# A graph aggregation with layer norm on one core: gathered rows split twice per four groups instead of four times, and the ring of copied indices taken out

## The chip, the cores and the metric

One core of one Trainium2 chip runs the kernel. The metric is device microseconds of one launch, the median of three runs; the program before takes 1273.84 us (1270.81 to 1276.02).

## The reference, cut to what matters

`x` has 100,000 rows of 128 float32, and there are 50,000 edges (`src`, `dst`). The output is a layer norm over each row of x plus the summed messages of its edges:

```python
row, col = (edge_index[0], edge_index[1])            # row = src, col = dst
messages = jnp.einsum('ei,oi->eo', x[col], W) + b
out = jax.ops.segment_sum(messages * agg_weight, row, num_segments=x.shape[0])
x = _layernorm(x + out, axis=-1)
```

So each edge adds row x[dst], times W, plus b, to node src. The sum over the rows is made first and multiplied by W after it, and b is added as often as the node has edges (its degree).

## The kernel before, in words

The first part of the program (about 244 us of the profiled span) sorts the edges into a **table** of 441 lists of up to 128 edges. Its last step, `decode` (L894 to L903), turns the sorted words into two int32 of each entry: the row of x to gather (`table[:, c, 0]`) and the node's column within a window (`table[:, c, 1]`). It does so for the first 36 lists (`head`), and then for the rest.

The second part goes over 196 **groups** of 512 nodes (the last one has fewer). Four groups are one **period**, and a period has 9 lists, so there are 49 periods. A list spans up to 308 nodes, so it can serve two neighbouring groups. The code calls g the group, u its place in a ring, m = period modulo RX (RX = 4) the ring place of the gathered rows. The engines work as follows.

- GpSimd (POOL) issues for each list one indirect DMA that gathers 128 rows of x into `xg[:, m, k]` (L516). The row numbers come from `now`, a ring of 4 periods that VectorE fills with a copy of 9 table entries (`fetch`, L968; the first four at L960). The copy for a period is made 13 rounds ahead of the period's first group and waits until the matmuls have released the ring place; POOL waits for the copy (`s_idx`).
- VectorE (DVE) splits the gathered float32 rows into three bf16 parts. The upper half of each word is the first part; `rest` = xg minus that part (L980); `xl` = rest minus rest's upper half (L985). Between these, one comparison for each list builds `sel` (L982), the 0/1 matrix of edges by nodes. These three steps are `select`. `CLASS` gives for each of a period's groups the lists that start there: 3, 2, 3 and 1. `select` runs once per group, for 384, 256, 384 and 128 columns, and up to 6 groups ahead of the group that is being finished (`lead`).
- TensorE (PE) sums the rows of each node: three matmuls for each list and group (L696, L698, L700), and for two groups at a time a degree matmul (L710), after which `s_agg` rises by 2. This is `aggregate`. `project`, two groups behind, adds b by degree (L723) and the product with W (L726), and signals `s_out`.
- ScalarE (ACT) copies the sums out of PSUM (L1094) and for every odd group the degrees of two groups (L1097); three groups behind it takes the square root (`std`, L1101), and four groups behind it writes the normalised output `y` (four instructions, L1107).
- VectorE's **round** g is: `add_x` (h = bank times aw plus x, 128x512, L991, waits for `s_out`), `select` for a later group, `moments` (four bn_stats of h, L997, which wait for h by `s_h`), `invert` of g - 1 (L1007, waits for ACT's std), `combine` (four bn_aggr, L1003), and `recentre` of g - 1 (L1011).
- SyncE loads x by group into `xt` and stores `y`, with rings of 8.

The order on each engine is that in which the code is written; the engines meet by semaphores alone. This is VectorE's order:

```python
lead = lambda g: min(6, 4 + g // 4)
for g in range(lead(0)):
    one(select, g)
for g in range(GA + 1):
    one(fetch, g + 13)
    one(add_x, g)
    for ahead in range(g + lead(g), g + 1 + lead(g + 1)):
        one(select, ahead)
    one(moments, g)
    one(invert, g - 1)
    one(combine, g)
    one(recentre, g - 1)
```

## Time and profile before

| what | value |
|---|---|
| median of three runs | 1273.84 us |
| span of the profiled execution | 898.2 us |
| around the span (median less span) | 375.6 us |
| first gather to the last | 245.2 to 855.5 us |
| DVE busy over the span | 853.2 us (95%) |
| PE / ACT / POOL busy | 735.0 / 656.6 / 592.8 us (82 / 73 / 66%) |
| granted TensorE clock, mean | 0.949 |

The profile gives the span from the first to the last instruction of one execution and no second time for the same execution; what the device time has beyond it is taken as the difference to the median. Two successive instructions of DVE overlap in the trace: the first one's duration reaches beyond the start of the second. So what an instruction costs its engine is read from start to start, and the duration only says when its result is there.

### The profile page before, as it was taken

How to read it: one execution, taken by the hardware profiler on the slowest of the kernel's cores; microseconds unless marked ns; L12 is line 12 of the kernel's file. 1: busy time of each engine (PE TensorE's matmuls, PEld its weight loads, DVE VectorE, ACT ScalarE, POOL GpSimd, SP SyncE). 2: the span in 40 equal slices, each digit the busy share in tenths (PEclk: the TensorE clock that was granted, in tenths of full speed). 3: DMA queues.
4: the chain of work that ended last, by engine and by line, in shares of the span. 5: the costliest groups of instructions: out<-in, count | busy, mean ns of one | idle time of the engine just before them, and what ended most of it. 6: DMA issues, size and time to landing. Idle time of an engine off the chain costs nothing.

```text
span 898.2 us, 24417 instructions
## 1 busy us (share of the span) xinstructions
PE 735.0 (82%) x7822; PEld 549.6 (61%) x7849; DVE 853.2 (95%) x3877; ACT 656.6 (73%) x1690; POOL 592.8 (66%) x601
## 2 busy tenths in 40 slices
PE   4889999999978778787877887879778787797874
PEld 3735555555456666666766676657666666675664
DVE  7989999999959999999999999999999999999997
ACT  2157777777526777777887778777777787878778
POOL 3047777776477777777777777776777777777710
PEclk9999999999999999989999999998999989989898
DMA  2001111110225677676666766676666666666653
GB/s 74 24 15 38 38 38 38 38 38 26 87 82 166 206 217 213 213 220 215 212 215 207 212 210 212 208 215 204 205 209 217 210 211 206 215 208 211 210 182 120
DMA packets 81035, 141.18 MB, mean 157 GB/s; under 512 B 19360, under 2 KB 20396, under 8 KB 80908
## 3 DMA queue, kind: packets, MB, share of 16 engines
q1 hardware_dynamic: 62476, 110.55, 36.7%
q0 software_dynamic: 18432, 29.08, 13.4%
q8 instruction: 63, 1.03, 0.5%
q14 instruction: 64, 0.52, 0.2%
HBM read 87.64 MB, written 51.92 MB: 155 GB/s over the span
## 4 chain that ended last, share of the span: by engine, by line
DVE 66%; PE 22%; issue 7%; ACT 2%; POOL 2%; DMA 0%; SPq 0%; ACTq 0%; DVEq 0%; POOLq 0%
DVE stats L997 16%; DVE h L991 11%; DVE sel L982 10%; PE bank L648 9%; DVE rest L980 8%; DVE xl L985 7%; DVE mv L1003 7%; PE bank L542 2%; PE bank L597 2%; PE bank L726 2%; PE bank L603 2%; ACT y L1107 1%; POOL xg L516 1%; PE bank L612 1%; DVE rstd L1007 1%
## 5 line engine op out<-in xcount | busy, mean ns | idle before, releaser
L516 POOL DMA_INDIRECT xg<-in_x,now x441 | 448.7, 1018 | 173.1 <-issue 132.5
L1107 ACT ACTIVATE y<-h,shift,rstd 128x128 f32<-128x128 f32 x784 | 320.2, 479 | 0.1
L726 PE MATMUL bank<-wT,aggT 128*128 128x128 f32 x1568 | 242.2, 301 | 0.0
L726 PEld LDWEIGHTS bank<-wT,aggT 128*128 128x128 f32 x1568 | 203.4, 203 | 28.4 <-issue 11.9
L696 PE MATMUL bank<-sel,xg 128*128 128x308 bf16 (+11 forms) x685 | 170.3, 261 | 7.6 <-DVE xl L985 7.6
L698 PE MATMUL bank<-sel,rest 128*128 128x308 bf16 (+11 forms) x685 | 176.4, 261 | 0.0
L479 POOL DMA_INDIRECT place_scratch<-word_col,place_row x135 | 135.7, 1005 | 55.4 <-issue 50.1
L997 DVE BATCH_NORM_STATS2 stats<-h 128x6 f32<-128x128 f32 x784 | 168.9, 275 | 0.2
L700 PE MATMUL bank<-sel,xl 128*128 128x308 bf16 (+11 forms) x685 | 166.9, 261 | 0.0
L1101 ACT ACTIVATE std<-mv,eps 128x4 f32<-128x4 f32 x196 | 58.3, 298 | 131.0 <-DVE mv L1003 130.9
L991 DVE SCALAR_TENSOR_TENSOR h<-bank,aw,xt 128x512 f32<-128x512 f32 x196 | 145.5, 742 | 6.3 <-PE bank L726 5.4
L723 PE MATMUL bank<-b,deg 32*128 32x128 bf16 x784 | 39.0, 215 | 120.0 <-ACT aggT L1094 119.9
L1094 ACT COPY aggT<-bank 128x512 f32<-128x512 f32 x196 | 110.3, 563 | 22.3 <-PE bank L700 22.3
L648 PE MATMUL bank<-oh_t,oh_s 128*128 128x441 bf16 x512 | 110.9, 354 | 2.6 <-ACT oh_s L1073 2.1
L982 DVE TENSOR_SCALAR sel<-iota_win,now 128x308 bf16<-128x308 f16 (+1 forms) x441 | 109.6, 294 | 0.0
L723 PEld LDWEIGHTS bank<-b,deg 32*128 32x128 bf16 x784 | 24.1, 92 | 129.8 <-ACT aggT L1094 128.7
L980 DVE TENSOR_TENSOR rest<-xg 128x384 f32<-128x384 f32 x196 | 87.3, 445 | 5.4 <-DMA xg<-in_x,now 5.2
L1073 ACT ACTIVATE oh_s<-oh_s,ratio_col 128x128 bf16<-128x128 bf16 x256 | 86.0, 396 | 7.3 <-DVE oh_s L875 4.4
L877 DVE TENSOR_SCALAR oh_t<-iota_nb,t_now 128x441 bf16<-128x441 f16 x256 | 87.8, 343 | 0.0
L985 DVE TENSOR_TENSOR xl<-rest 128x384 bf16<-128x384 f32 x196 | 87.4, 446 | 0.0
L875 DVE TENSOR_SCALAR oh_s<-iota_nb,slot,word_col 128x128 bf16<-128x128 f16 x256 | 86.8, 339 | 0.0
L696 PEld LDWEIGHTS bank<-sel,xg 128*128 128x128 bf16 x685 | 70.2, 103 | 18.9 <-DVE xl L985 8.7
(153 smaller groups left out, 938.3 us busy)
## 6 DMA issues: line engine op xcount, KB each, us to landing
xt<-in_x SPq DMA_DIRECT2D x195, 256.0 KB, 3.8
out<-y SPq DMA_DIRECT2D x195, 256.0 KB, 2.6
xg<-in_x,now POOLq DMA_INDIRECT x441, 3.8
hi_row<-hi_scratch SPq DMA_DIRECT2D x50, 128.0 KB
place_scratch<-word_col,place_row POOLq DMA_INDIRECT x135
place_scratch<-scattered SPq DMA_DIRECT2D x1, 441.0 KB, 3.6
scattered<-place_scratch SPq DMA_DIRECT2D x1, 441.0 KB, 3.2
src_rows<-in_src SPq DMA_DIRECT2D x1, 192.0 KB
```

The source lines that it names most:

```text
L516: nc.gpsimd.indirect_dma_start(out=xg[:, m, k], out_offset=None, in_=x, in_offset=bass.IndirectOffsetOnAxis(ap=now[:, m, k, 0:1], axis=0)) ...
L648: last = nc.tensor.matmul(TABLES[w][:, 0:NB], hot, oh_t[:, no % RING], start=(no == 0), stop=False, skip_group_check=True)
L696: nc.tensor.matmul(AGG[q][:, nodes], top[:, ring, k, :, 1], sel[:, half, k, cols], start=(i == 0), stop=False, skip_group_check=True)
L698: nc.tensor.matmul(AGG[q][:, nodes], middle[:, half, k, :, 1], sel[:, half, k, cols], start=False, stop=False, skip_group_check=True)
L700: last = nc.tensor.matmul(AGG[q][:, nodes], xl[:, half, k], sel[:, half, k, cols], start=False, stop=(i == len(lists) - 1), skip_group_che ...
L726: last = nc.tensor.matmul(OUT[u % RO][:, nodes[j]], aggT[:, u % RO, nodes[j]], wT[:], start=False, stop=True, skip_group_check=True)
L980: V.tensor_tensor(rest[:, m % 2, lists], xg[:, m, lists], top[:, m, lists, :, 1], ALU.subtract).then_inc(s_upper, 1)
L982: V.tensor_scalar(sel[:, m % 2, k, 0:WIDTH[k]], iota_win[:, WIN[k]:WIN[k] + WIDTH[k]], now[:, m, k, 1:2], None, ALU.is_equal).then_inc(s_s ...
L985: V.tensor_tensor(xl[:, m % 2, lists], rest[:, m % 2, lists], middle[:, m % 2, lists, :, 1], ALU.subtract).then_inc(s_lower, 1)
L991: V.scalar_tensor_tensor(h[:, u].rearrange("p j d -> p (j d)"), OUT[u % RO][:], aw[:], xt[:, u].rearrange("p j d -> p (j d)"), ALU.mult, A ...
L997: V.bn_stats(stats[:, u, j], h[:, u, j]).then_inc(s_stats, 1)
L1107: nc.scalar.activation(y[:, u, j], h[:, u, j], ACT.Identity, bias=shift[:, u, j:j + 1], scale=rstd[:, u, j:j + 1]).then_inc(s_y, 1)
```

## The change

- `CLASS` becomes `HALVES`: lists 0 to 4 (which serve the period's first two groups) and lists 5 to 8. `select` now runs twice a period, on 640 and on 512 columns, with five and with four `sel` comparisons. VectorE runs the first two before round 0, then the third in round 0, the fourth in round 1, and from round 2 on one in every even round (`after_add`): in round g it is half g // 2 + 3. Odd rounds have none.
- `now` is gone, with `fetch` and the first four copies. The gathers and the comparisons read `table` itself.
- POOL waits for `s_idx` (1 when the first 36 lists are decoded, 2 when all are) and, from the fifth period on, for `s_agg`, which says that the ring place is free. `s_agg` is PE's own signal; VectorE no longer stands between.
- The waits of `select` and `aggregate` are counted in halves, and the separate semaphore for list 0 goes.

```diff
-    CLASS = [[k for k in range(LISTS) if max(FIRST[k] - TAIL, 0) // GN == u] for u in range(SPAN_G)]
+    HALVES = [[k for k in range(LISTS) if max(FIRST[k] - TAIL, 0) // GN // 2 == half] for half in range(2)]
...
-                def gather(g, u, n, period, m, mn):
-                    if u % SPAN_G == 0:
-                        pool.wait_ge(s_idx, period + 1)
+                def gather(period, m):
+                    pool.wait_ge(s_idx, 1 if period < RX else 2)
+                    pool.nop(nofuse=True)
+                    if period >= RX:
+                        pool.wait_ge(s_agg, (period - RX + 1) * SPAN_G)
                         pool.nop(nofuse=True)
...
-                                in_offset=bass.IndirectOffsetOnAxis(ap=now[:, m, k, 0:1], axis=0)
+                                in_offset=bass.IndirectOffsetOnAxis(ap=table[:, period * LISTS + k, 0:1], axis=0)
...
-                for period in range(RX):
-                    V.tensor_copy(now[:, period].rearrange("p k w -> p (k w)"),
-                                  table[:, period * LISTS:period * LISTS + LISTS].rearrange("p k w -> p (k w)")).then_inc(s_idx, 1)
-                decode(head, NB)
-
-                def fetch(g, u, n, period, m, mn):
-
-                    if u % SPAN_G == 0 and not (g < RX * SPAN_G):
-                        at_least(dve, s_agg, g - (RX - 1) * SPAN_G)
-                        V.tensor_copy(now[:, m].rearrange("p k w -> p (k w)"),
-                                      table[:, bass.ds(period * LISTS, LISTS)].rearrange("p k w -> p (k w)")
-                                      ).then_inc(s_idx, 1)
-
-                def select(g, u, n, period, m, mn):
-                    dve.wait_ge(s_idx, period + 1)
-                    at_least(dve, s_agg, g - (SPAN_G + 2))
-                    mine = CLASS[u % SPAN_G]
+                decode(head, NB).then_inc(s_idx, 1)
+
+                def select(half_no):
+
+                    period, half = half_no // 2, half_no % 2
+                    m, mn = period % RX, period // RX
+                    mine = HALVES[half]
                     lists = slice(mine[0], mine[-1] + 1)
-                    if u % SPAN_G == 0:
-                        dve.wait_ge(s_first[m], 16 * mn + 16)
-                    dve.wait_ge(s_rest[m][u % SPAN_G], (16 * mn + 16) * len([k for k in mine if k]))
+                    at_least(dve, s_agg, 2 * half_no - 4)
+                    dve.wait_ge(s_rows_in[m][half], (16 * mn + 16) * len(mine))
...
-                lead = lambda g: min(6, 4 + g // 4)
-                for g in range(lead(0)):
-                    one(select, g)
+                after_add = {g: g // 2 + 3 for g in range(2, 4 * PERIODS, 2) if g // 2 + 3 < 2 * PERIODS} | {0: 2, 1: 3}
+                select(0)
+                select(1)
                 for g in range(GA + 1):
-                    one(fetch, g + 13)
                     one(add_x, g)
-                    for ahead in range(g + lead(g), g + 1 + lead(g + 1)):
-                        one(select, ahead)
+                    if g in after_add:
+                        select(after_add[g])
```

Here is VectorE's order before at the start of the second part: the selections of the third and fourth group of period 0, then round 0's `add_x` and its selection of three lists of period 1.

```order
L982 TENSOR_SCALAR sel<-iota_win,now 128x307
L985 TENSOR_TENSOR xl<-rest 128x256 [waits s_upper]
L980 TENSOR_TENSOR rest<-xg 128x384 [waits s_rest0_2,s_idx]
L982 TENSOR_SCALAR sel<-iota_win,now 128x308
L982 TENSOR_SCALAR sel<-iota_win,now 128x307
L982 TENSOR_SCALAR sel<-iota_win,now 128x308
L985 TENSOR_TENSOR xl<-rest 128x384 [waits s_upper]
L980 TENSOR_TENSOR rest<-xg 128x128 [waits s_rest0_3,s_idx]
L982 TENSOR_SCALAR sel<-iota_win,now 128x307
L985 TENSOR_TENSOR xl<-rest 128x128 [waits s_upper]
L991 SCALAR_TENSOR_TENSOR h<-bank,aw,xt 128x512 [waits s_x0,s_out]
L980 TENSOR_TENSOR rest<-xg 128x384 [waits s_rest1_0,s_first1,s_idx]
```

And the same place of VectorE now.

```order
L973 TENSOR_TENSOR xl<-rest 128x640 [waits s_upper]
L967 TENSOR_TENSOR rest<-xg 128x512 [waits s_rows_in0_1]
L970 TENSOR_SCALAR sel<-iota_win,table 128x308 [waits s_idx]
L970 TENSOR_SCALAR sel<-iota_win,table 128x307
L970 TENSOR_SCALAR sel<-iota_win,table 128x308
L970 TENSOR_SCALAR sel<-iota_win,table 128x307
L973 TENSOR_TENSOR xl<-rest 128x512 [waits s_upper]
L979 SCALAR_TENSOR_TENSOR h<-bank,aw,xt 128x512 [waits s_x0,s_out]
L967 TENSOR_TENSOR rest<-xg 128x640 [waits s_rows_in1_0]
L970 TENSOR_SCALAR sel<-iota_win,table 128x308 [waits s_idx]
L970 TENSOR_SCALAR sel<-iota_win,table 128x308
L970 TENSOR_SCALAR sel<-iota_win,table 128x307
```

The second selection before round 0 now covers lists 5 to 8 at once and waits for all four; round 0's selection waits for five lists of period 1, where it waited for three.

The second place is VectorE in the steady part, in the round of an even group behind its `add_x`, up to the copy ahead of the next one, before.

```order
L980 TENSOR_TENSOR rest<-xg 128x384 [waits s_first0,s_rest0_0,s_agg,s_idx]
L982 TENSOR_SCALAR sel<-iota_win,now 128x308 x2
L982 TENSOR_SCALAR sel<-iota_win,now 128x307
L985 TENSOR_TENSOR xl<-rest 128x384 [waits s_upper]
L997 BN_STATS stats<-h 128x6 [waits s_h]
L997 BN_STATS stats<-h 128x6 x3
L1007 RECIPROCAL rstd<-std 128x4 [waits s_std]
L1003 BN_AGGR mv<-stats 128x2 [waits s_stats]
L1003 BN_AGGR mv<-stats 128x2 x3
L1011 SCALAR_TENSOR_TENSOR shift<-mv,rstd 128x4 [waits s_rstd]
L968 COPY now<-table 128x18 [waits s_agg]
```

And an odd round of VectorE now, with the beginning of the even round behind it.

```order
L979 SCALAR_TENSOR_TENSOR h<-bank,aw,xt 128x512 [waits s_x3,s_out]
L985 BN_STATS stats<-h 128x6 [waits s_h]
L985 BN_STATS stats<-h 128x6 x3
L995 RECIPROCAL rstd<-std 128x4 [waits s_std]
L991 BN_AGGR mv<-stats 128x2 [waits s_stats]
L991 BN_AGGR mv<-stats 128x2 x3
L999 SCALAR_TENSOR_TENSOR shift<-mv,rstd 128x4 [waits s_rstd]
L979 SCALAR_TENSOR_TENSOR h<-bank,aw,xt 128x512 [waits s_x4,s_out]
L967 TENSOR_TENSOR rest<-xg 128x512 [waits s_rows_in2_1,s_agg]
L970 TENSOR_SCALAR sel<-iota_win,table 128x308 [waits s_idx]
```

In the odd round the `rest`, `sel` and `xl` that stood between `add_x` and the first bn_stats are gone, and the bn_stats that waits for h now follows directly behind the instruction that writes h; the copy into `now` is gone too.

## Rows read from the trace of the kernel before

**Rows 1.** View by windows, six stretches of the second part, summed: busy us (instructions).

```profile
sum 606.54, PE 485.82 PEld 402.73 DVE 599.65 ACT 478.04 POOL 428.55; mean PE 80.97 PEld 67.12 DVE 99.94 ACT 79.67 POOL 71.42
```

**Rows 2.** View of waits, DVE, 271.5 to 878 us: total, times, longest.

```profile
DVE mv L1003 <- issue: 1.1, 5, 0.4
```

**Rows 3.** Timeline of DVE, steady part: start us, duration, instruction.

```profile
606.64 0.28 DVE L980 TENSOR_TENSOR rest<-xg 128x128 f32<-128x128 f32 x1
606.84 0.29 DVE L982 TENSOR_SCALAR sel<-iota_win,now 128x307 bf16<-128x307 f16 x1
...
608.58 0.74 DVE L991 SCALAR_TENSOR_TENSOR h<-bank,aw,xt 128x512 f32<-128x512 f32 x1
609.24 0.54 DVE L980 TENSOR_TENSOR rest<-xg 128x384 f32<-128x384 f32 x1
609.71 0.71 DVE L982 TENSOR_SCALAR sel<-iota_win,now 128x308 bf16<-128x308 f16 x3
610.34 0.55 DVE L985 TENSOR_TENSOR xl<-rest 128x384 bf16<-128x384 f32 x1
...
612.11 0.17 DVE L968 COPY now<-table 128x18 int32<-128x18 int32 x1
612.19 0.74 DVE L991 SCALAR_TENSOR_TENSOR h<-bank,aw,xt 128x512 f32<-128x512 f32 x1
```

**Rows 4.** Timeline of DVE, the last rounds, which have no selection.

```profile
881.17 0.74 DVE L991 SCALAR_TENSOR_TENSOR h<-bank,aw,xt 128x512 f32<-128x512 f32 x1
...
883.28 0.75 DVE L991 SCALAR_TENSOR_TENSOR h<-bank,aw,xt 128x512 f32<-128x512 f32 x1
884.06 0.87 DVE L997 BATCH_NORM_STATS2 stats<-h 128x6 f32<-128x128 f32 x4
...
888.17 0.75 DVE L991 SCALAR_TENSOR_TENSOR h<-bank,aw,xt 128x512 f32<-128x512 f32 x1 [0.38 <-PE bank L726]
```

**Rows 5.** Groups of DVE, 293.44 to 872.68 us: busy, mean ns, idle before.

```profile
L991 DVE SCALAR_TENSOR_TENSOR h<-bank,aw,xt 128x512 f32<-128x512 f32 x181 | 134.3, 742 | 0.5 <-issue 0.5
```

**Rows 6.** Timeline of DVE, start of the second part.

```profile
258.11 0.55 DVE L985 TENSOR_TENSOR xl<-rest 128x384 bf16<-128x384 f32 x1
...
261.27 0.75 DVE L991 SCALAR_TENSOR_TENSOR h<-bank,aw,xt 128x512 f32<-128x512 f32 x1 [2.00 <-PE bank L726]
262.38 0.56 DVE L980 TENSOR_TENSOR rest<-xg 128x384 f32<-128x384 f32 x1 [0.36 <-DMA xg<-in_x,now]
...
263.52 0.55 DVE L985 TENSOR_TENSOR xl<-rest 128x384 bf16<-128x384 f32 x1
...
268.35 0.75 DVE L991 SCALAR_TENSOR_TENSOR h<-bank,aw,xt 128x512 f32<-128x512 f32 x1 [3.02 <-PE bank L726]
...
279.22 0.75 DVE L991 SCALAR_TENSOR_TENSOR h<-bank,aw,xt 128x512 f32<-128x512 f32 x1
```

**Rows 7.** Timeline of POOL, start: gathers of lists 8, 11 and 22.

```profile
255.63 0.95 POOL L516 DMA_INDIRECT xg<-in_x,now  x1 [0.30 <-issue]
...
259.79 0.95 POOL L516 DMA_INDIRECT xg<-in_x,now  x1 [0.30 <-issue]
...
274.01 0.95 POOL L516 DMA_INDIRECT xg<-in_x,now  x1 [0.30 <-issue]
```

**Rows 8.** Page, DMA issues: count, median us from issue to landing.

```profile
xg<-in_x,now POOLq DMA_INDIRECT x441, 3.8
```

**Rows 9.** Groups of POOL, 293 to 872 us.

```profile
L516 POOL DMA_INDIRECT xg<-in_x,now x405 | 412.3, 1018 | 151.9 <-issue 111.2 <-DVE now L968 40.6
```

**Rows 10.** Timeline of ACT, steady part: every std of three rounds.

```profile
602.50 0.30 ACT L1101 ACTIVATE std<-mv,eps 128x4 f32<-128x4 f32 x1 [0.83 <-DVE mv L1003]
...
606.04 0.30 ACT L1101 ACTIVATE std<-mv,eps 128x4 f32<-128x4 f32 x1 [0.76 <-DVE mv L1003]
...
608.63 0.30 ACT L1101 ACTIVATE std<-mv,eps 128x4 f32<-128x4 f32 x1 [0.28 <-DVE mv L1003]
```

**Rows 11.** Timeline of PE, same stretch: degree and bias matmuls of a pair of groups.

```profile
605.38 0.40 PE L723 MATMUL bank<-b,deg 32*128 32x128 bf16 x8 [1.85 <-ACT aggT L1094]
```

35 lines of the change are left out of this document (16 added, 19 removed).

## The prediction

> **What bounds the kernel now.** I read the busy time by windows first. Over the second part, 271 to 878 us, the sum has DVE busy for 599.65 of 606.54 us, with PE, ACT and POOL at 80, 79 and 71% [rows 1]. The reader is to see one full engine and three with room. The view of waits then has to show that DVE waits for nobody: its largest entry there is 1.1 us, for its own issue [rows 2]. No entry names another engine. So in this stretch time is DVE's sum from start to start, and a change is worth what it does to that sum, until another engine becomes later. The mean pace is 180 rounds in 579.24 us, 3.22 us a round or 12.87 us a period [rows 5]. Ahead of it lies a start in which DVE does wait, for PE and for gathers [rows 6], and there the order of lists counts, not the sum.
>
> **What an instruction costs DVE.** From start to start, `rest` on 384 columns takes 609.71 - 609.24 = 0.47 us and on 128 columns 606.84 - 606.64 = 0.20 us [rows 3]. So 128 columns take 0.13 us, and 0.07 us is the fixed part of one instruction (0.135 and 0.065 before rounding; I take 0.066). `xl` costs the same as `rest` (its 0.55 us duration at 384 is equal), and a `sel` costs (610.34 - 609.71) / 3 = 0.21 us. A copy into `now` costs 612.19 - 612.11 = 0.08 us [rows 3]. No row has 640 or 512 columns. By the line they take 0.73 and 0.60 us; the bounds are 0.66 (the 512-column `add_x`, with its longer lead) and 0.93 us for 640 columns (two of 384), and I take the line, since nothing in it bends between 128 and 384.
>
> **The steady part, step by step.** I count from the `add_x` of round 4, where the start is over.
> - Fewer instructions. Before, 187 selections are left there; now 93 halves. That is 94 fewer `rest` and 94 fewer `xl`, 188 x 0.066 = -12.4 us. Columns and comparisons stay (9 lists a period).
> - Copies. 44 of the 45 are left, 44 x 0.08 = -3.5 us.
> - What the selection covered. Before, `add_x` is followed by `rest`, which does not need h, and the start to start is 609.24 - 608.58 = 0.66 us [rows 3]. Where no selection stands there, the bn_stats that waits for h starts 884.06 - 883.28 = 0.78 us behind `add_x` [rows 4]. The last six rounds of the kernel before run so. Now every odd round does: rounds 5 to 189 are 93 rounds, 93 x 0.12 = +11.2 us. This term takes back nine tenths of the first.
>
> The sum is -4.7 us, 0.1 us a period: the pace should go from 12.87 to 12.77 us. Every one of the three terms lies on DVE, in the stretch where it waits for nothing, so each counts in full.
>
> On the third term the Trainium skill says otherwise. In "VectorE: DVE Perf Modes", section "The DRAIN you can't avoid", chained operations with a semaphore after each took as long as without, "the semaphore costs nothing extra here". By that, the term would be nothing and the steady sum -15.9 us. The rows of this kernel show 0.78 against 0.66, so the trace does not agree, at least for this pair, and I go by it.
>
> **The start.** Before, PE's third aggregation needs the three lists 5 to 7, whose `xl` ends at 258.11 + 0.55 = 258.66, and `add_x` of round 0 comes 2.61 us later, at 261.27 [rows 6]. Now it needs lists 5 to 8. List 8 is issued at 255.63 [rows 7]. From issue to use it took 262.38 - 259.79 = 2.6 us for list 11 [rows 6, 7], and gathers begin some 0.3 us earlier, as the first release no longer waits for a copy (one takes 0.17 us [rows 3]; 0.2 to 0.4 with its signal, my choice in the middle). So the half starts at 255.63 - 0.3 + 2.6 = 257.9 and its `xl` ends 0.60 + 4 x 0.21 + 0.68 = 2.1 us later, at 260.1 (0.68: the duration, 0.55 and one more 0.13). `add_x` of round 0 comes at 262.7, 1.4 us late. The next half waits for list 13, two gathers of 0.95 + 0.30 us behind list 11 [rows 7]: 259.79 + 2.5 - 0.3 + 2.6 = 264.6. It takes 0.73 + 5 x 0.21 + 0.81 = 2.6 us, to 267.2; before, the end was 263.52 + 0.55 = 264.1, and `add_x` of round 1 came 4.3 us behind, at 268.35 [rows 6]. Now it comes at 271.5. A round without selection is 883.28 - 881.17 = 2.11 us [rows 4]; with four lists it is 0.66 + 0.60 + 0.84 + 0.60 + 1.33 = 4.0, with five 4.5 us. Round 1 ends at 275.5. Round 2 wants list 22, issued at 274.01 [rows 7], there at 276.3 to 277.5 (2.6 us as above, or the median landing of 3.8 us [rows 8]), and wants it at 276.2: 0.1 to 1.3 us of waiting, I take 0.5. Rounds 2 and 3 end at 275.5 + 4.5 + 0.5 + 2.1 = 282.6. Before, round 4 began at 279.22 [rows 6], but with 21 lists selected, and now it is 23; the two are worth 2 x (0.21 + 2 x 0.13) = 0.9 us of later work. So the start costs 282.6 - 279.2 - 0.9 = **+2.4 us** (1.5 to 3.5).
>
> **Sum.** -4.7 + 2.4 = -2.3 us, 1273.84 - 2.3 = **1271.5 us**. The sum is made on the profiled span of 898.2 us; the 375.6 us around it are taken as they are. The three runs before lie between 1270.81 and 1276.02, so the forecast is within their spread. A change under 0.5%, 6.4 us, can't be told from none.
>
> **Why the other edits cost nothing, and what covers them.** Gathers: 9 a period take (412.3 + 111.2) / 45 = 11.6 us, and the other 40.6 us of POOL's idle time was spent on VectorE's copy, 0.9 us a period [rows 9]. PE's `s_agg` now releases them some rounds earlier; the pace stays that of DVE, with 12.77 - 11.6 = 1.1 us left. Without that room every gather over 1.42 us would show in full. Uneven rounds: now DVE takes 4.3 us, then 2.1, where it took 3.2 each. ACT's work per round is 606.04 - 602.50 - 0.76 = 2.8 us with the degree copy and 608.63 - 606.04 - 0.28 = 2.3 us without [rows 10]. In the short round ACT does the kind without: it falls behind by 0.2 us, and the long round has 1.5 us to spare over 2.8. DVE asks for the std of the long round 0.78 + 0.78 = 1.5 us into the short one, and ACT has it after 0.3. PE's bias matmuls start when ACT's degree copy is done, at 605.38 here [rows 11], and the `add_x` that waits for the product behind them came at 608.58 [rows 3], 3.2 us later. In the new rhythm the three rounds ahead of such an `add_x` are 8.5 us where they were 9.7, so 1.2 of these 3.2 us go. PE's whole work for a group is some 2.6 us (80% of 3.22 [rows 1]), and bias and product are a part of it, by my estimate half, 1.3 us; so about 0.7 us stays.
>
> **Rivals.**
> - *The dependence is free* (0.10). By the skill's rule on chained operations, or if wait and write overlap otherwise here, the 11.2 us don't come: -15.9 + 2.4 = -13.5 us, **1260 us**. Against it stand the six last rounds, all with the long gap.
> - *The short rounds come too soon* (0.07, slower). Place: `add_x` of an even group behind a short round, waiting for PE. In the last rounds before, which are short one behind the other, three took 888.17 - 881.17 = 7.0 us where 6.3 were needed, and the wait for PE at their end is 0.38 us [rows 4]. If each of the 93 pairs had that wait, it would be +35 us, less 2.3: **1306 us**. It decides when PE or ACT is later by the 0.7 us above, for instance with the granted clock at the 1.2 GHz level in that part of most pairs. Against it: long rounds stand between, and ACT catches up in each.
> - *Gathers bound* (0.03). If the 9 gathers took over 12.8 us, each 0.1 us a gather beyond would be 0.9 us a period, +40 us. Mean and idle time [rows 9] speak against it; an excess of 0.015 us a gather would end at **1278 us**.
> - *The sum as worked out* has 0.80, its own range 1265 to 1279: start 1.5 to 3.5; DVE's own short issue gaps [rows 2] may go or double, some 2 us; runs scatter by 2.6 us either way. Of it 0.05 lies beyond 0.5% faster and 0.02 beyond 0.5% slower.
>
> That the change does not happen is excluded: the order of instructions shows halves and no copies.
>
> **Range and chances.** 1264 to 1280 us leaves out the first two rivals and a little of the rest, some 0.19. Faster 0.05 + 0.10 = 0.15; slower 0.02 + 0.07 + 0.01 = 0.10; same 0.75.
>
> **What would show it.** Right: DVE has under 10 us of waits for others between 280 and 870 us; `rest` at 640 columns takes 0.73 us to the next start; odd rounds are 2.11 us, pairs 6.4; `add_x` of odd rounds to bn_stats 0.78 us; round 0 and round 1 start at 262.7 and 271.5. Wrong: a gap of 0.66 there (first rival); DVE idle before `add_x` named PE, once a pair (second); POOL without any wait for `s_agg` and DVE waiting for gathers in the steady part (third). The sum is also wrong if the wide `rest` costs more than the line, each 0.05 us of it being 10 us over 188 instructions.

## The result, and the profile after

The changed kernel takes 1357.6 us (median of four runs, 1354.5 to 1363.47), the kernel before 1272.66 us beside it (1270.81 to 1276.02). The ratio is 1.0662, 95% interval 1.0615 to 1.0709: the change costs 85 us, and the forecast of 1271.5 us was wrong.

One thing has to be known to read the two profiles side by side. The page of before (span 898.2 us) can't be of an execution like the timed ones: a timed execution takes 1.7 to 2.8 us more than its span in every run below, so this one took some 900 us and not 1273. In the experiments the same kernel takes 898 us on some chips and 1254 to 1277 us on others. I call the first kind a free chip and the second a held one, by what TensorE does there. By this the page of before is from a free chip, and the timed runs and the page after (1363.47 us, span 1361.7) are from a held one.

The page of the changed kernel: span, the engines' busy time, the granted clock, and two of its costliest groups (busy, mean ns of one | idle time before them).

```profile
span 1361.7 us, 24068 instructions
PE 910.3 (67%) x7822; PEld 623.6 (46%) x7849; DVE 847.9 (62%) x3632; ACT 655.3 (48%) x1690; POOL 572.7 (42%) x601
...
PEclk9867788888956776787787678777877777787789
...
L517 POOL DMA_INDIRECT xg<-in_x,table x441 | 427.7, 970 | 539.7 <-PE bank L708 395.8
L979 DVE SCALAR_TENSOR_TENSOR h<-bank,aw,xt 128x512 f32<-128x512 f32 x196 | 146.4, 747 | 352.3 <-remote 272.7
```

VectorE has less work than before (3,632 instructions), and is busy for 62% of the span. Its `add_x` (L979) waits 352 us in all, where it waited 0.5 us over most of the second part in [rows 5]. GpSimd is no bound either: it waits 395.8 us for PE's degree matmul (L708), which is the new release, where [rows 9] had 40.6 us for VectorE's copy. No engine is full. Waits of TensorE in the steady part of the same kernel, 450 to 1250 us (total, times, longest):

```profile
PE bank L696 <- issue: 63.1, 78, 1.9
PE bank L694 <- issue: 59.5, 78, 1.8
PE bank L698 <- issue: 56.0, 80, 1.8
PE bank L721 <- ACT aggT L1081: 55.3, 42, 5.3
```

TensorE's three aggregation matmuls stand idle "for issue", that is for nothing that the profile shows. The timelines of GpSimd, TensorE and VectorE in one period of the same kernel show when:

```profile
700.18 0.95 POOL L517 DMA_INDIRECT xg<-in_x,table  x1 [8.03 <-PE bank L708]
...
710.26 0.95 POOL L517 DMA_INDIRECT xg<-in_x,table  x1 [0.30 <-issue]
...
720.26 0.95 POOL L517 DMA_INDIRECT xg<-in_x,table  x1 [9.05 <-PE bank L708]
```

```profile
704.96 0.21 PE L694 MATMUL bank<-sel,xg 128*128 128x114 bf16 x1
...
705.93 0.21 PE L696 MATMUL bank<-sel,rest 128*128 128x114 bf16 x1 [0.76 <-issue]
706.67 0.21 PE L698 MATMUL bank<-sel,xl 128*128 128x114 bf16 x1 [0.53 <-issue]
707.41 0.29 PE L694 MATMUL bank<-sel,xg 128*128 128x308 bf16 x1 [0.53 <-issue]
```

```profile
711.00 0.75 DVE L979 SCALAR_TENSOR_TENSOR h<-bank,aw,xt 128x512 f32<-128x512 f32 x1 [7.61 <-remote]
```

The burst of nine gathers begins at 700.18 and its last issue is at 710.26. From 705 us, five behind its begin, TensorE starts one matmul each 0.73 us, with some 0.5 us of nothing between; VectorE's `add_x` then waits 7.6 us. The next burst begins 20.1 us after this one. Over rounds 8 to 188 a period takes 19.5 us, where the page of before has 12.87 [rows 5].

The results turn late before the starts turn slow. ScalarE's copy of a group's sums at 713.18 us waits for the aggregation matmul that the trace has done by 703.64:

```profile
703.40 0.24 PE L698 MATMUL bank<-sel,xl 128*128 128x193 bf16 x1
```

```profile
713.18 0.59 ACT L1081 COPY aggT<-bank 128x512 f32<-128x512 f32 x1 [7.86 <-remote]
```

I set each such copy beside its matmul. In rounds 8 to 187 of this trace 44 copies start over 2 us behind the recorded end, 8.9 us on average, and their matmuls began from 3.2 us behind the first gather of a burst on; so do 46 `add_x` behind their product matmuls, from 2.3 us on. In the traces of free chips (before, e1, e5) there are none. So what TensorE started from some 2 to 3 us into a burst on comes out only when the burst is over, and from 5 us on its starts are slow too. I call both the **hold**. The view by windows of the same stretch shows how few matmuls start meanwhile (columns: window, its length, then busy us and number of instructions of PE, PEld, DVE, ACT and POOL, the granted clock, the DMA share, GB/s):

```profile
701.00:703.00 2.00, 2.00 (x26) 1.73 (x24) 1.94 (x12) 1.72 (x5) 1.39 (x3) 1.00 0.18 60
703.00:705.00 2.00, 2.00 (x21) 1.54 (x19) 0.39 (x5) 2.00 (x7) 1.60 (x2) 1.00 0.61 180
705.00:707.00 2.00, 0.60 (x5) 0.19 (x2) 0.00 (x0) 0.32 (x1) 1.47 (x2) 1.00 0.82 259
707.00:709.00 2.00, 0.74 (x4) 0.31 (x4) 0.00 (x0) 0.00 (x0) 1.39 (x2) 1.00 0.75 243
709.00:711.00 2.00, 0.34 (x3) 0.12 (x2) 0.00 (x0) 0.00 (x0) 1.69 (x2) 0.52 0.29 80
711.00:713.00 2.00, 0.74 (x4) 0.39 (x3) 2.00 (x5) 0.00 (x0) 0.21 (x1) 0.50 0.12 33
```

TensorE goes from 26 and 21 matmuls in 2 us to 5, 4 and 3. The granted clock is still 1.00 (2.4 GHz) when that begins and falls to 0.50 (1.2 GHz) at 709.1 us, four microseconds into the slow starts. So in this period the low clock follows the hold; it doesn't make it. It lasts to 719.3 us, so it may add to the loss behind the hold; no run separates that.

### The profile page after: what moved, and what is told of

It reads as the page before. It is cut to its first block, busy times and chain, and to the rows that moved or that the text cites. A ratio compares the mean times of both kernels' runs of the same rounds, so it can differ in the third digit from the quotient of the medians.

```text
span 1361.7 us, 24068 instructions
## 1 busy us (share of the span) xinstructions
PE 910.3 (67%) x7822; PEld 623.6 (46%) x7849; DVE 847.9 (62%) x3632; ACT 655.3 (48%) x1690; POOL 572.7 (42%) x601
## 3 DMA queue, kind: packets, MB, share of 16 engines
q1 hardware_dynamic: 62476, 110.55, 24.5%
## 4 chain that ended last, share of the span: by engine, by line
DVE 33%; another core or an unknown queue 28%; PE 22%; issue 9%; ACT 7%; ACTq 0%; DMA 0%; POOL 0%; SPq 0%; DVEq 0%; POOLq 0%
PE bank L650 9%; DVE stats L985 8%; DVE sel L970 5%; DVE h L979 5%; PE bank L724 4%; DVE rest L967 4%; DVE mv L991 4%; DVE xl L973 3%; ACT y L1094 3%; PE bank L544 1%; ACT aggT L1081 1%; ACT same_hi L1040 1%; ACT oh_s L1060 1%; PE bank L589 1%
## 5 line engine op out<-in xcount | busy, mean ns | idle before, releaser
L517 POOL DMA_INDIRECT xg<-in_x,table x441 | 427.7, 970 | 539.7 <-PE bank L708 395.8
L979 DVE SCALAR_TENSOR_TENSOR h<-bank,aw,xt 128x512 f32<-128x512 f32 x196 | 146.4, 747 | 352.3 <-remote 272.7
L724 PE MATMUL bank<-wT,aggT 128*128 128x128 f32 x1568 | 283.1, 332 | 14.3 <-issue 14.0
L724 PEld LDWEIGHTS bank<-wT,aggT 128*128 128x128 f32 x1568 | 237.9, 231 | 45.9 <-issue 34.7
L698 PE MATMUL bank<-sel,xl 128*128 128x308 bf16 (+11 forms) x685 | 189.3, 287 | 60.2 <-issue 59.9
L650 PE MATMUL bank<-oh_t,oh_s 128*128 128x441 bf16 x512 | 141.0, 427 | 21.3 <-ACT oh_s L1060 9.3
L696 PEld LDWEIGHTS bank<-sel,rest 128*128 128x128 bf16 x685 | 77.2, 113 | 108.6 <-issue 90.4
L698 PEld LDWEIGHTS bank<-sel,xl 128*128 128x128 bf16 x685 | 75.7, 110 | 90.2 <-issue 76.8
L873 DVE TENSOR_SCALAR oh_s<-iota_nb,slot,word_col 128x128 bf16<-128x128 f16 x256 | 86.2, 337 | 32.2 <-PE bank L650 18.1
L970 DVE TENSOR_SCALAR sel<-iota_win,table 128x308 bf16<-128x308 f16 (+1 forms) x441 | 102.3, 298 | 0.0
L1040 ACT ACTIVATE same_hi<-bank 128x512 bf16<-128x512 f32 x100 | 55.5, 594 | 71.6 <-remote 66.3
L650 PEld LDWEIGHTS bank<-oh_t,oh_s 128*128 128x128 bf16 x512 | 52.0, 112 | 82.1 <-issue 51.3
```

The lines of the kernel that those rows point to most:

```text
L517: nc.gpsimd.indirect_dma_start(out=xg[:, m, k], out_offset=None, in_=x, in_offset=bass.IndirectOffsetOnAxis(ap=table[:, period * LISTS + k ...
L650: last = nc.tensor.matmul(TABLES[w][:, 0:NB], hot, oh_t[:, no % RING], start=(no == 0), stop=False, skip_group_check=True)
L696: nc.tensor.matmul(AGG[q][:, nodes], middle[:, half, k, :, 1], sel[:, half, k, cols], start=False, stop=False, skip_group_check=True)
L698: last = nc.tensor.matmul(AGG[q][:, nodes], xl[:, half, k], sel[:, half, k, cols], start=False, stop=(i == len(lists) - 1), skip_group_che ...
L724: last = nc.tensor.matmul(OUT[u % RO][:, nodes[j]], aggT[:, u % RO, nodes[j]], wT[:], start=False, stop=True, skip_group_check=True)
L970: V.tensor_scalar(sel[:, m % 2, k, 0:WIDTH[k]], iota_win[:, WIN[k]:WIN[k] + WIDTH[k]], table[:, period * LISTS + k, 1:2], None, ALU.is_equ ...
```

## The experiments

The expectations stand as written before each run. Two names recur: "halves" is the half of the change that selects twice a period, and "table" the half that reads the decoded table and lets `s_agg` release the gathers. e1 to e9 ran on free chips, e10 to e12 and all s-runs on held ones.

**e1: the kernel before once more, unchanged.** Is it 1273 us, or 898 with 375 somewhere?

> The kernel before, unchanged. The changed kernel's time and span are 2 us apart, while the page of before has a span of 898.2 us for a time of 1272 us. Theory A (the profiled execution of before was of another kind than its timed ones, and these have stretches in which TensorE issues slowly, as the changed kernel has): a fresh profile shows a span of about 1270 us, a granted clock near 0.8, and TensorE rows with idle time put down to issue. Theory B (375 us lie around the span, and the change alone brought the slow stretches): the span is 898 us again and the clock 0.95.

898.43 us (median of ten), beside 898.4 for the kernel before. The profiled execution took 900.07 us with a span of 898.1, so 2 us lie around a span and not 375, and Theory B falls. The span of 1270 us that Theory A forecast did not come either, but its first half is borne out: the page of before and the recorded 1272.66 us are of executions of different kinds. Why they differ this run can't show; s1 has the profile that Theory A asked for.

**e2: the halves alone** (the changed kernel, with the copies into `now` and their release put back).

```diff
+    pool.wait_ge(s_idx, period + 1)
-    if period >= RX:
-        pool.wait_ge(s_agg, (period - RX + 1) * SPAN_G)
...
-    ap=table[:, period * LISTS + k, 0:1]
+    ap=now[:, m, k, 0:1]
...
+    one(fetch, g + 13)
```

> The changed kernel with the ring of copied indices put back: gathers wait for VectorE's copy, selections stay in halves of five and four lists. Theory H (the halves make the loss: two short and two long rounds, and later lists at the start): about 1357 us. Theory T (reading the table and the release by the matmuls' own signal make it, since gathers then go out early and in bursts): about 1270 us. If both share: between, near 1315 us.

901.07 us, ratio 1.003 (1.0019 to 1.0041). On a free chip neither this run nor e3 tests the two theories, since there is no loss to share; s3 and s4 do.

**e3: the table alone** (the kernel before, with the reads and the release of the changed one).

```diff
+    if period >= RX:
+        pool.wait_ge(s_agg, (period - RX + 1) * SPAN_G)
...
-    ap=now[:, m, k, 0:1]
+    ap=table[:, period * LISTS + k, 0:1]
...
-    one(fetch, g + 13)
```

> The kernel before with one part of the change: gathers and comparisons read the table, the ring is gone, gathers are released by the matmuls' signal; selections stay four a period. Theory T: about 1357 us. Theory H: about 1270 us, 3 us less by the copies.

894.92 us, ratio 0.9954 (0.9936 to 0.9972): -3.5 us, as the 44 copies at 0.08 us of the prediction; the interval allows -2.5 to -5.7.

**e4: plain loads** (the kernel before, with each gather replaced by a load of 128 rows that lie together).

```diff
-    nc.gpsimd.indirect_dma_start(out=xg[:, m, k], out_offset=None, in_=x,
-        in_offset=bass.IndirectOffsetOnAxis(ap=now[:, m, k, 0:1], axis=0))
+    first = (period * LISTS + k) * P
+    nc.gpsimd.dma_start(out=xg[:, m, k], in_=x[first:first + P, :])
```

> The kernel before with each indirect gather replaced by a plain load of 128 consecutive rows from the same engine, so that rows of x are not those of the edges; same bytes. Theory S (TensorE's slow stretches come with GpSimd's indirect transfers): the second part runs at VectorE's pace of 12.9 us a period, the slow stretches stay in the sorting part alone, where scatters remain, and the time falls to about 1000 us. Theory E (they have nothing to do with them): within 2% of 1272 us.

893.03 us, ratio 0.9937 (0.9919 to 0.9956). The kernel sums rows that are not those of the edges. On a free chip it hardly matters how the rows come, so this run says nothing of the recorded result; s2 is the same kernel on a held chip.

**e5: the changed kernel once more, unchanged.**

> The changed kernel, unchanged. Here the kernel before runs in 898.4 us, halves alone in 901.1 and the table alone in 894.9. Theory C (the 1357.6 and 1272.7 us belong to a condition of the chip in which TensorE issues slowly, and the change's own work is what halves and table sum to): 898.4 + 2.7 - 3.5 = 897.6 us, within 1 us. Theory D (the slow stretches belong to the changed kernel, as both parts together): well over 950 us, and slow stretches again.

898.26 us beside 897.63, ratio 1.0003 (0.9993 to 1.0014). On this chip the change is worth nothing that can be measured, which is what the prediction said. Page and steady timeline of VectorE in this run:

```profile
span 894.5 us, 24068 instructions
PE 733.4 (82%) x7822; PEld 545.4 (61%) x7849; DVE 844.2 (94%) x3632; ACT 647.6 (72%) x1690; POOL 582.7 (65%) x601
```

```profile
599.25 0.74 DVE L979 SCALAR_TENSOR_TENSOR h<-bank,aw,xt 128x512 f32<-128x512 f32 x1
599.91 0.68 DVE L967 TENSOR_TENSOR rest<-xg 128x512 f32<-128x512 f32 x1
600.51 0.93 DVE L970 TENSOR_SCALAR sel<-iota_win,table 128x308 bf16<-128x308 f16 x4
...
603.27 0.74 DVE L979 SCALAR_TENSOR_TENSOR h<-bank,aw,xt 128x512 f32<-128x512 f32 x1
604.04 0.88 DVE L985 BATCH_NORM_STATS2 stats<-h 128x6 f32<-128x128 f32 x4
...
605.37 0.74 DVE L979 SCALAR_TENSOR_TENSOR h<-bank,aw,xt 128x512 f32<-128x512 f32 x1
```

The round with four lists takes 603.27 - 599.25 = 4.02 us, the short one 605.37 - 603.27 = 2.10, and `add_x` to bn_stats is 0.77 us where no selection stands between.

**e6: halves, but spread over both rounds.** From half 5 on, the odd round does `rest` and two comparisons, and the even round the other comparisons and `xl`; so `add_x` has work behind it in every round.

```diff
...
+    elif g % 2 and (g + 7) // 2 < 2 * PERIODS:
+        begin((g + 7) // 2, 2)
+    elif g % 2 == 0 and (g + 6) // 2 < 2 * PERIODS:
+        finish((g + 6) // 2, 2)
```

> The changed kernel with each half spread over two rounds from the fifth half on: the odd round does rest and two comparisons, the even round behind it the other comparisons and xl, so that each add_x has an instruction behind it that does not wait for h. Theory G (the 0.12 us between add_x and bn_stats in 93 odd rounds take back what fewer instructions save): 11 us less than the changed kernel, about 887 us, with a period of 12.47 us. Rival F (the dependence costs nothing, or the wide rest costs more than the line says): no change against the changed kernel.

885.42 us, ratio 0.9856 (0.9839 to 0.9873), 12.8 us less than the changed kernel of e5, and a period of 12.53 us over rounds 8 to 188. This is about the 11.2 us of the third term come back: of the versions run on free chips it is the fastest, 1.4% below the kernel before.

**e7: release by half** (the changed kernel; the gathers of a period's second half wait for two groups more).

```diff
-    pool.wait_ge(s_agg, (period - RX + 1) * SPAN_G)
     for half in range(2):
+        pool.wait_ge(s_agg, (period - RX + 1) * SPAN_G + 2 * half)
```

> The changed kernel, with GpSimd's gathers released by halves: the five of the first half as now, the four of the second only when the matmuls are two groups further. In the profile that came with the result, all of TensorE's slow stretches begin four or more gathers into a burst of nine and end some 3 us behind it. Theory P (bursts of back-to-back gathers hold TensorE off, in a condition of the chip that not every run has): where the kernel before runs in 898 us, no difference to it (897 to 899 us); where it runs in 1272 us, bursts of five and four cost less than one of nine, at least 3 us a period, and this kernel is under 1220 us. Theory Q (the slow stretches come from something else that only coincides): in that condition 1357 us as the changed kernel.

896.51 us beside 898.06 for the kernel before, ratio 0.9975 (0.9963 to 0.9987), half a microsecond below the range. On a free chip the theories don't differ; on a held chip this kernel was not run, so its question stays open.

**e8: nothing behind `add_x`** (the kernel before, with the selection moved behind the four bn_stats, in every round).

```diff
     one(add_x, g)
+    one(moments, g)
     for ahead in range(g + lead(g), g + 1 + lead(g + 1)):
         one(select, ahead)
-    one(moments, g)
     one(invert, g - 1)
```

> The kernel before, with every selection moved behind the four bn_stats of its round, so that in all of the 190 rounds that have one, the first bn_stats stands directly behind the add_x that it waits for. Theory G (0.12 us each): 190 x 0.12 = 23 us more than before, 921 us. Rival F (the dependence is free): no change. A little of it could be hidden in the first rounds, where VectorE waits anyway.

891.49 us, ratio 0.9923 (0.9906 to 0.994), 30 us less than the theory gave. The gap is there as forecast; another one went. Timeline of VectorE, first in e1 (selection ahead of the bn_stats), then in e8:

```profile
604.52 0.87 DVE L997 BATCH_NORM_STATS2 stats<-h 128x6 f32<-128x128 f32 x4
605.30 0.16 DVE L1007 RECIPROCAL rstd<-std 128x4 f32<-128x4 f32 x1
605.49 0.38 DVE L1003 BATCH_NORM_AGGREGATE mv<-stats 128x2 f32<-128x6 f32 x4
605.78 0.14 DVE L1011 SCALAR_TENSOR_TENSOR shift<-mv,rstd 128x4 f32<-128x4 f32 x1
```

```profile
601.68 0.74 DVE L991 SCALAR_TENSOR_TENSOR h<-bank,aw,xt 128x512 f32<-128x512 f32 x1
602.46 0.88 DVE L997 BATCH_NORM_STATS2 stats<-h 128x6 f32<-128x128 f32 x4
...
603.85 0.18 DVE L1007 RECIPROCAL rstd<-std 128x4 f32<-128x4 f32 x1
603.94 0.35 DVE L1003 BATCH_NORM_AGGREGATE mv<-stats 128x2 f32<-128x6 f32 x4
604.20 0.13 DVE L1011 SCALAR_TENSOR_TENSOR shift<-mv,rstd 128x4 f32<-128x4 f32 x1
```

`add_x` to bn_stats grows from 0.66 to 0.78 us. But bn_aggr, which reads what bn_stats wrote, starts 0.09 us behind the reciprocal where it started 0.19 behind it, and is through after 0.26 us where it took 0.29. So 0.12 - 0.10 - 0.03 is about nothing, and the selection had only moved its cover from one dependent pair to the other. Summed from start to start over rounds 20 to 180, e8 against e1: `add_x` to its successor +19.0 us, reciprocal to bn_aggr -16.0, between the bn_aggr -6.1, `recentre` to the next `add_x` -1.3; 4.2 us less in all, of the 6.6 us between the medians.

**e9: cover for both pairs** (e6, with each round's share cut in two, one piece ahead of the bn_stats and one behind).

```diff
...
+    elif g % 2 and (g + 7) // 2 < 2 * PERIODS:
+        remainders((g + 7) // 2)
+    elif g % 2 == 0 and (g + 6) // 2 < 2 * PERIODS:
+        compare((g + 6) // 2, 2, 9)
     one(moments, g)
+    if g > 2 and g % 2 and (g + 7) // 2 < 2 * PERIODS:
+        compare((g + 7) // 2, 0, 2)
+    elif g > 2 and g % 2 == 0 and (g + 6) // 2 < 2 * PERIODS:
+        lower((g + 6) // 2)
```

> Halves spread over two rounds as in the spread kernel, and each round's share cut in two: one piece between add_x and the bn_stats, one between the bn_stats and the reciprocal. In the run with selections behind the bn_stats, the step from reciprocal to the first bn_aggr was 0.09 us where it is 0.18 us elsewhere, and the occasional 0.25 us gaps among the bn_aggr were gone. Theory G2 (both results, h and the statistics, cost a wait where they are asked for at once, and a piece of selection hides either): 190 x 0.09 = 17 us less than the spread kernel's 885.4, and some 6 us of gaps less, 862 to 868 us. Rival K (the next bound is near: GpSimd needs 11.6 us for a period's gathers, ScalarE 5.1 us for a pair): it ends at 875 to 885 us, with VectorE waiting for TensorE or for gathers. In the condition in which the kernel before takes 1272 us: no less than 1300 us, since VectorE is not the bound there.

888.59 us beside 897.79, ratio 0.9893 (0.9875 to 0.9911). Waits of VectorE in e9, 300 to 880 us:

```profile
DVE rest L966 <- DMA xg<-in_x,table: 29.3, 34, 3.0
```

Both ranges of the expectation were missed, and e6 is 3 us faster. The gain for VectorE came (reciprocal to bn_aggr 0.09 us on average), but now it waits for gathers: between 300 and 880 us GpSimd waits for the release for 0.6 us only. Nine gathers take it 12.7 us here and not the 11.6 us of the prediction, since one issue takes 1102 ns on average where it takes 1005 in e6. So the bound that Rival K names is met, at a higher price than it gives.

**e10, e11, e12: TensorE held by hand.** These were built to copy the hold on a free chip: TensorE waits at one aggregation a period until the nine gathers of a burst have landed, in the changed kernel (e10) and in the kernel before at the third (e11) and the fourth group (e12). This is e10's edit; the other two wait for the same gathers by their own semaphores.

```diff
+    held = (g + 10) // SPAN_G
+    if (g + 10) % SPAN_G == 0 and held < PERIODS:
+        for half in range(2):
+            pe.wait_ge(s_rows_in[held % RX][half], (16 * (held // RX) + 16) * len(HALVES[half]))
```

> The changed kernel with TensorE held by hand as its slow profile shows it: at the aggregation of each period's third group it waits until the nine gathers that are being issued then have landed (and at the very first one for the 36 of the start). In the slow profile it stands still from some 5 us behind the first gather of a burst to some 3 us behind the last. Theory P2 (that hold alone makes the second part's slow pace): first gather to add_x of round 8 some 95 us, then 19 to 20.5 us a period as in that profile (19.5 us), together about 290 us more than the changed kernel free, near 1200 us. Theory Q2 (the slow clock and slow issue between holds matter as much): 17 us a period or less, under 1100 us.

> The kernel before with the same hold at the same place of TensorE's order, the third group. Here VectorE releases the burst, later in TensorE's order than in the changed kernel, so that this place may come less than 5 us behind a burst's first gather. Theory R (the release by VectorE's copy makes the burst overlap with other waits, so the same hold costs less): 17 to 18.5 us a period, as the time of 1272 us would want where the changed kernel takes 1357. Theory R2 (the release makes no difference to a hold): as the held changed kernel within 0.3 us a period.

> The kernel before with the hold one group later in TensorE's order, at the fourth. Of the two places the one that TensorE reaches some 5 us behind the first gather of the burst is the one that answers to the slow condition; this is read from the trace. Theory R: the one that fits runs at 17 to 18.5 us a period. Theory R2: at 19 us or more.

They ran on a held chip, where the kernel before takes 1253.96 us: 1381.69, 1727.84 and 1608.06 us (one run each), with a burst every 20.5, 28.2 and 25.6 us. The hold by hand came on top of the chip's own. In e10 TensorE's long wait begins 5 us into the burst, as was meant, but in e12 with the burst and in e11 3 us ahead of it. So they don't answer the question as asked. They show one thing: about the same hold by hand takes e10 to 128 us above the kernel before, 43 more than the change alone, and the kernel before itself 354 to 474 us up, by which group it falls on and how far the burst has gone.

**s1: the kernel before, unchanged, on a held chip.** With it there is a trace of before to hold beside the one of after.

> The kernel before, unchanged, for its profile in the condition in which it takes some 1260 us (on any other chip this run repeats the first experiment and says nothing new). Theory P (in that condition TensorE is held off from the fifth gather of a burst to 3 us behind the last): slow stretches in its rows too, as many as bursts, the start held until the first 36 gathers are out, and a period of 17 to 18.5 us. Theory W (its gathers do no harm, the clock does): no such stretches, TensorE busy throughout at a lower granted clock.

1277.34 us beside 1275.42, ratio 1.0057 (0.9996 to 1.0117). Its page, and TensorE's waits from 450 to 1150 us:

```profile
span 1278.9 us, 24417 instructions
PE 895.1 (70%) x7822; PEld 633.3 (50%) x7849; DVE 856.8 (67%) x3877; ACT 660.2 (52%) x1690; POOL 591.0 (46%) x601
```

```profile
PE bank L723 <- issue: 82.4, 39, 4.2
PE bank L710 <- issue: 67.4, 102, 1.2
```

The kernel before is held too, with a period of 17.8 us, as Theory P has it, and Theory W falls. But here the hold falls on the degree matmuls (L710) and the bias (L723), and not on the aggregation. The view by windows, 5 to 14 us behind the begin of two bursts, first in s1 and then in the changed kernel (columns as above):

```profile
705.00:714.00 9.00, 5.70 (x33) 4.22 (x34) 4.11 (x23) 3.22 (x9) 5.10 (x6) 0.76 0.51 161
723.00:732.00 9.00, 4.71 (x35) 3.20 (x36) 4.16 (x23) 2.77 (x9) 5.19 (x6) 0.89 0.52 162
```

```profile
705.20:714.20 9.00, 2.45 (x11) 1.11 (x11) 3.20 (x9) 1.14 (x3) 4.77 (x5) 0.72 0.42 133
725.20:734.20 9.00, 2.62 (x13) 0.75 (x10) 3.89 (x12) 1.49 (x4) 4.77 (x5) 0.74 0.48 145
```

TensorE starts 33 and 35 matmuls in these 9 us, and after the change 11 and 13; GpSimd's part, five or six issues, is about the same. In e1, on a free chip, it starts 82 on average in the same place of a burst: the kernel before loses most of them too, and the change loses half of the rest. The late results are there as well: 55 copies of sums start over 2 us late, by 7.6 us on average. Where the 83 us lie, by stage (us; the first column is when the first gather is issued, the others are stretches between `add_x` of the rounds named):

| | first gather | to round 0 | to round 8 | rounds 8 to 188 | to the end | span |
|---|---|---|---|---|---|---|
| e1, before, free chip | 242.9 | 16.1 | 32.2 | 581.5 | 25.5 | 898.1 |
| e5, changed, free chip | 241.3 | 19.1 | 32.0 | 576.4 | 25.6 | 894.4 |
| s1, before, held chip | 360.9 | 53.5 | 38.7 | 800.2 | 25.5 | 1278.9 |
| changed, held chip | 361.0 | 54.3 | 42.8 | 878.1 | 25.6 | 1361.7 |
| s5, held chip | 345.8 | 40.4 | 43.1 | 795.8 | 25.5 | 1250.6 |
| s6, held chip | 352.5 | 20.6 | 55.9 | 782.0 | 24.5 | 1235.6 |

Of the 82.8 us between s1 and the changed kernel, 77.9 lie in rounds 8 to 188, and none in the sorting.

**s2: e4 on a held chip.** Do the indirect transfers make the hold?

> The kernel before with plain loads of consecutive rows in place of the indirect gathers (rows of x that are not those of the edges). In the slow condition, Theory P: TensorE's slow stretches are gone from the second part and stay in the sorting part, which keeps its scatters, so the time falls to 1000 to 1050 us. Theory W: 1250 us, as the kernel before.

1014.69 us (two runs), ratio 0.7953 (0.7878 to 0.8028). Its page:

```profile
span 1016.8 us, 24417 instructions
PE 773.1 (76%) x7822; PEld 562.3 (55%) x7849; DVE 849.5 (84%) x3877; ACT 659.0 (65%) x1690; POOL 378.1 (37%) x601
```

Rounds 8 to 188 take 578.4 us, as on a free chip (800.2 in s1), and no copy of sums is late. Theory P holds. The first part still takes 366.9 us, and it still has indirect transfers, its scatters. So the hold comes with the indirect transfers. The edit changes two things at once, though: the rows lie together, and GpSimd needs 4.8 us for nine issues where nine indirect ones take it 11 to 12. Which of these does it is not shown.

**s3 and s4: e3 and e2 on a held chip.** Which half of the change is it?

> The kernel before with the table read itself and gathers released by the matmuls' signal, selections four a period. In the slow condition, Theory R3 (the release makes the loss: a burst starts right behind the signal of the matmuls and holds them off at once): 1340 us or more. Theory H3 (the halves make it: the uneven rounds add to the hold): within 1% of the kernel before.

> The changed kernel with the ring of copied indices and VectorE's release put back. In the slow condition, Theory H3: 1340 us or more. Theory R3: within 1% of the kernel before.

Table alone: 1359.26 us, ratio 1.0653 (1.0623 to 1.0684), the whole loss, as Theory R3 says. Halves alone: 1322.41 us, ratio 1.0365 (1.031 to 1.0419); both expectations for the halves missed (two runs each). The two don't add up. In the traces, 5 to 14 us behind the begin of a burst (all bursts between 450 and 1250 us) TensorE starts on average 14.5 matmuls with the table alone, 27.8 with the halves alone, 33.8 in s1 and 16.1 with both, and the burst returns after 19.9, 19.0, 17.9 and 19.8 us.

**s5: the table, released late.** e3 again, with the release put back to about the round in which VectorE's copy used to give it (`s_rstd` rises by 2 with each round).

```diff
     pool.wait_ge(s_agg, (period - RX + 1) * SPAN_G)
+    pool.wait_ge(s_rstd, 2 * (4 * period - 14))
```

> The table-only kernel with one more wait of GpSimd before each period's gathers: for the end of the VectorE round before the one in which the copy used to be made, so that a burst begins where it began in the kernel before. Where the kernel before takes some 1270 us, Theory R4 (the place of the release decides): 1265 to 1285 us, down from 1359. Theory T4 (reading the table, or the layout, decides): 1350 us or more. Where the kernel before takes 898 us: 895 us either way, as the table-only kernel.

1258.56 us beside 1257.94, ratio 0.9993 (0.9961 to 1.0025); the range stated was for a chip on which the kernel before takes 1270. One line takes the 6.5% away again; 35.2 matmuls start in the 9 us, and the burst returns after 17.7 us. The line does what it says: a burst begins 15.4 us behind the degree matmul that frees its ring place, 15.7 in s1, and 0.8 in s3 and in the changed kernel. Reading the table costs nothing. The place of the release costs all that the table part costs.

**s6: e6 with the same line.**

> The halves spread over two rounds (885.4 us where the kernel before takes 898) with the same later release. Where the kernel before takes some 1270 us: by the halves-only run, which lost 3.7% with the release at the old place, and since VectorE's savings are not on the path there, 1290 to 1325 us if the uneven order of selections is what cost there, and 1265 to 1285 us if an even order heals it. Where the kernel before takes 898 us: 884 to 887 us.

1237.34 us (three runs) beside 1257.94, ratio 0.984 (0.9782 to 0.9897), below both ranges of the expectation. On a held chip this is the fastest version run, with 38.6 matmuls in the 9 us and a burst every 17.5 us. It was not run on a free chip, nor e6 on a held one, so what the spread and the late release do apart is not shown.

## Why the prediction was wrong

**The step that failed first: "the 375.6 us around it are taken as they are".** Only some 2 us lie around a span: e1's profiled execution has 900.07 us with a span of 898.1, the changed kernel's 1363.47 us with a span of 1361.7. An execution of 898 us and a median of 1273.84 couldn't be of one condition, and the prediction laid the sum of one on the time of the other. All that it read (DVE full, PE at 80%) is true of a free chip alone. On a held chip VectorE is at 67% already before the change (s1), and DVE's sum decides nothing.

**The step that failed by it: "PE's `s_agg` now releases them some rounds earlier; the pace stays that of DVE".** The release was seen and priced at nothing, with GpSimd's spare time as the only cover asked for. On a held chip what counts is not whether the gathers come in time, but what TensorE has to do while they are issued. With the copy, the burst began 15.7 us behind the degree matmul that frees the ring place (s1), and of the slow steps of TensorE's starts (0.66 to 0.78 us, from 365 us on) 65 of 85 led to a degree matmul. Released by `s_agg`, it begins 0.8 us behind (700.18 above), and TensorE is then in the aggregation of the next groups: 115 of 120 slow steps led to an aggregation matmul, 16 matmuls start where 34 did, the late copies of sums and `add_x` start 8.9 and 7.8 us behind their matmuls on average (7.6 and 5.6 in s1), and the period grows from 17.8 to 19.5 us. s3 (the release alone has the whole loss), s5 (the release moved back, nothing lost) and s2 (no indirect transfers, no hold) show that the place of the release decides and that the hold comes with the gathers. Why the same hold costs more at one place than at the other is read from the traces only.

**The steps that held, on a free chip.** The pace was forecast to go from 12.87 to 12.77 us a period; over rounds 20 to 180 it went from 12.88 (e1) to 12.81 (e5). That is -3.1 us over the steady part for the -4.7 of the sum. (Rounds 8 to 188 give -5.1 against e1 and -2.8 against the page of before: two executions of one kernel differ by as much as the term.) The copies at 3.5 us agree with e3's -3.5. The uncovered `add_x` cost 0.11 us in e5 (0.775 against 0.661 on average) for the 0.12, and e6 got it back by giving each `add_x` a piece of selection. The prediction weighed against it the Trainium skill's "the semaphore costs nothing extra here" ("VectorE: DVE Perf Modes", section "The DRAIN you can't avoid"). That sentence compares one chain of copies with and without semaphores; the rows here compare an instruction that needs the result ahead of it with one that doesn't. No run here has the skill's comparison, so the two don't contradict each other. The 640-column `rest` took 0.73 us to the next start, by the line. Round 0 came 3.0 us later behind the first gather, where 1.4 was said, and round 4 3.3 us later, where 3.4 was said; less the 0.9 us of later work this is the 2.4. The medians differ by +0.63 us (-0.6 to +1.3 by the interval) for -2.3, a small miss and still under the 0.5% that the prediction calls none.

**The rivals.** "The dependence is free" fell: 0.77 us, not 0.66 (e5). "The short rounds come too soon" fell on free chips: 0.3 us of waits for PE from 271 to 870 us. "Gathers bound" fell for this kernel, and was right for e9. None of them had the mechanism that decided.

**A step beyond, that e8 showed incomplete.** I took 0.12 us as a cost of one pair. The sum of a round depends on both pairs, `add_x` to bn_stats and bn_stats to bn_aggr, and moving the same cover from one to the other costs nothing (e8).

**What stays open.** Why some chips hold TensorE and others don't, and whether it is the chip at all or a condition of the time: no chip was met in both kinds, but each of the three held ones was met only once. Whether the gathers' issue or their traffic holds it: late results come out up to 3 us behind the last issue, with the transfers; the packets themselves take as long in either kind (0.13 us on average in e1 and in the changed kernel). Why the halves alone cost 3.7% on a held chip: 27.8 matmuls against 33.8 is a count and no cause. Their bursts begin 18.1 us behind the release's matmul and not 15.7, so the place may be at work there too; no run tests it. And whether splitting the release by half (e7) helps there.

## What to carry to other kernels

Hold the span of a profiled execution against its own time and against the median before you build on it: if they differ by much more than the 2 us seen here, profile and time are not of the same condition, and a sum from the one says nothing of the other. A signal that lets a burst of transfers go sets what the burst collides with; when an edit moves such a signal, even "only earlier" and with spare time on the issuing engine, ask what the other engines do during the burst. A piece of independent work between an instruction and its reader covers one wait, so spread such pieces over the rounds instead of gathering them. And before you trust a matmul's recorded end, look when the engine that waits for it starts.

## What the runs showed of the hardware that was not expected

- On some chips TensorE starts often only one instruction per 0.66 to 0.78 us from about 5 us behind the first of a run of indirect transfers until some 3 us behind the last. Of 120 such steps in the second part of the changed kernel's trace 98 begin within 1.3 us of a gather's issue, none more than 4 us from one, and none in the first 4 us of a burst; e1 has none at all.
- What TensorE started from 2.3 us behind the first gather on is late for its readers by up to 10 us there (the 44 copies and 46 `add_x` above). At the start, with 36 gathers back to back, the copy of the degrees starts at 411.87 us, 38 us behind the recorded end of the degree matmuls (374.0), and the bias matmul waits for it:

```profile
388.04 0.25 PE L694 MATMUL bank<-sel,xg 128*128 128x114 bf16 x1 [14.04 <-issue]
...
412.59 0.61 PE L721 MATMUL bank<-b,deg 32*128 32x128 bf16 x8 [22.64 <-ACT deg L1084]
```

- The same program takes 898 us on three chips and 1254 to 1277 us on three others, and 893 and 1015 us if its gathers are plain loads.
- The granted clock is 0.96 over e1 and 0.808 over s1. In the period shown of the changed kernel it falls where TensorE is held, after the slow starts have begun.
- A VectorE instruction that follows the one it depends on starts about 0.1 us later than one that doesn't: 0.78 us against 0.66 for `add_x` to bn_stats (e8, e1), and 0.19 against 0.09 for the reciprocal to bn_aggr when bn_stats stands right ahead (e1, e8).
- An indirect gather's issue has no fixed price: 1005 ns on average in e6 and 1102 ns in e9, with the same gathers.
